# First attention head group of a float32 decoder layer: context blocks first, K and V of a block in turn, first Q from unsplit float32 operands

## The reference, cut to what matters

```
q = layernorm(x) @ wq          # 128 x 4096: 32 query heads of 128, in 8 groups of 4
k = ctx @ wk ; v = ctx @ wv    # 2048 x 1024: one K head and one V head per group
q, k = rope(q), rope(k)        # ctx enters without a norm
scores = q @ k.T + mask ; probs = softmax(scores) ; x = x + (probs @ v) @ wo
```

## Time and profile before

| what | us |
|---|---|
| median of 3 executions (706.46 to 709.02) | 707.11 |
| the profiled execution, its own time | 707.14 |
| its span, first to last instruction | 705.4 |
| TensorE busy in that span | 694.2 (98%) |

### The profile page before, as it was taken

How to read it: one execution, slowest core, us unless ns; L and a number is a source line. 1 busy time by engine, 2 the same in 40 slices (tenths; PEclk the granted TensorE clock), 3 DMA queues, 4 the chain that set the end, 5 groups by cost and what they waited for, 6 DMA issues and landing times. The chain is left out here.

```text
span 705.4 us, 12247 instructions
## 1 busy us (share of the span) xinstructions
PE 694.2 (98%) x4088; PEld 592.4 (84%) x4088; DVE 547.5 (78%) x1180; ACT 391.9 (56%) x601; POOL 299.6 (42%) x151
## 2 busy tenths in 40 slices
PE   8999999999999999999999999999999999999997
PEld 7888888888888888888888888799989898999976
DVE  5988578658748857775874884867999999999984
ACT  4563454536546456454553654553867676767752
POOL 3353223404503513240450440300288887888762
PEclk9999999999999999999999999999999999999999
DMA  9602022021001202202101100781678888788710
GB/s 319 269 28 76 1 74 74 0 74 59 15 15 59 74 0 74 74 0 74 59 15 39 73 22 0 274 355 64 239 270 301 323 306 334 295 334 304 280 52 16
DMA packets 20293, 93.77 MB, mean 133 GB/s; under 512 B 2608, under 2 KB 3760, under 8 KB 11440
## 3 DMA queue, kind: packets, MB, share of 16 engines
q1 hardware_dynamic: 20272, 93.50, 36.0%
HBM read 93.17 MB, written 0.33 MB: 133 GB/s over the span
## 5 line engine op out<-in xcount | busy, mean ns | idle before, releaser
L1562 POOL TENSOR_TENSOR wqo_lo<-wqo_raw,wqo_hi 128x2048 fp32r<-128x2048 f32 x14 | 65.0, 4641 | 163.8 <-ACT wqo_hi L797 163.8
L1230 DVE TENSOR_TENSOR pt_lo<-bank,pt_hi 128x512 fp32r<-128x512 f32 x128 | 87.8, 690 | 48.5 <-ACT pt_hi L875 47.7
L875 ACT ACTIVATE pt_hi<-bank 128x512 fp32r<-128x512 f32 x128 | 75.8, 599 | 54.5 <-PE bank L521 48.9
L1549 POOL TENSOR_TENSOR k_lo<-rope_a,k_hi 128x512 fp32r<-128x512 f32 x32 | 42.7, 1336 | 103.9 <-ACT k_hi L815 103.9
L1595 POOL TENSOR_TENSOR w_out_lo<-w_out_sb,w_out_hi 128x2048 fp32r<-128x2048 f32 x16 | 73.4, 4588 | 21.6 <-ACT w_out_hi L986 21.6
L1138 DVE CUSTOM_DVE_ANT_0 probs<-bank,mask_sb 128x512 f32<-128x512 f32 x128 | 82.0, 685 | 0.1
L1600 POOL TENSOR_TENSOR w_gate_lo<-w_gate_sb,w_gate_hi 128x2048 fp32r<-128x2048 f32 x14 | 64.7, 4623 | 16.7 <-ACT w_gate_hi L978 16.7
L858 ACT ACTIVATE probs<-probs,neg_max 128x2048 f32<-128x2048 f32 x31 | 61.9, 2002 | 3.1 <-DVE neg_max L1128 3.1
L521 PEld LDWEIGHTS bank<-ident_r,probs_r 128*128 128x128 f32 x448 | 48.6, 139 | 15.7 <-DVE pt_lo L1230 3.3
L395 PE MATMUL bank<-pt_hi,v_hi 128*128 128x512 f32 (+1 forms) x144 | 61.0, 424 | 0.0
L655 PE MATMUL bank<-xnT,w_hs_sb 128*128 128x128 f32 x512 | 60.6, 277 | 0.0
(11 more groups left out here) (210 smaller groups left out, 1746.6 us busy)
## 6 DMA issues: line engine op xcount, KB each, us to landing
w_hs_sb<-in_w_hs SPq DMA_DIRECT2D x16, 1024.0 KB, 4.9
w_out_sb<-in_w_out SPq DMA_DIRECT2D x16, 1024.0 KB, 6.3
w_gate_sb<-in_w_gate SPq DMA_DIRECT2D x16, 1024.0 KB, 4.8
wqo_raw<-in_wq SPq DMA_DIRECT2D x8, 1024.0 KB, 4.8
wqo_raw<-in_wo SPq DMA_DIRECT2D x8, 1024.0 KB, 4.8
decay<-decay_rows SPq DMA_DIRECT2D x16, 512.0 KB, 6.8
ctx_raw<-in_ctx_t SPq DMA_DIRECT2D x3, 1024.0 KB, 11.2
wk_raw<-in_wk SPq DMA_DIRECT2D x8, 256.0 KB, 2.5
```

The source lines that it names most:

```text
L875: act.activation(pt_hi[t % 3], ring_b[(t + 1) % 2][:, :], ACT.Copy).then_inc(s["pt_hi_ready"], 1)
L1230: dve.tensor_tensor(pt_lo[t % 3], ring_b[(t + 1) % 2][:, :], pt_hi[t % 3].bitcast(F32), ALU.subtract)\
L1562: pool.tensor_tensor(wqo_lo[:, :, :], wqo_raw[:, :, :], wqo_hi[:, :, :].bitcast(F32), ALU.subtract)\
```

## The change

- **Transfers.** x moves from first place to behind the context's block 1 and the K rope tables 0. wq moves from third place to behind block 3. Block 0 comes in 4 pieces, blocks 1 to 3 in 2 pieces each, wv right after block 0.
- **Weights of group 0.** `wk` and `wv` are split by ACT (`hi`) and DVE (`lo`) in place of POOL. `wq` isn't split at all: Q of group 0 is 4 full float32 matmuls of `xnT` by `wqo_raw`, into another bank.
- **Norm.** Its statistics, scale and transposes move behind K2; the second run of 14 fillers goes, and the first shrinks from 32 to 20.
- **Order on TensorE.** K0 V0 K1 V1 K2, transposes of the norm, V2, a wait for `qx_lo` (the split norm that later groups use), V transposes 0, Q, K3, Q transposes, V transposes 1, V3, V transposes 2. The bank into which the norm is transposed is the one that V transposes 0 write, hence the wait.
- **Order on VectorE and ScalarE** follows this.

The diff's core (renamed semaphores and declarations left out):

```diff
@@ sync
-            sp.dma_start(xres[:, :], x).then_inc(s["x_in"], 16)
             sp.dma_start(wk_raw[:, :, :], wk[0]).then_inc(s["wk_in"], 16)
...
-            for i, two in enumerate(PAIRS):
-                sp.dma_start(ctx_raw[:, 0, two, :], ctx_t[:, two, 0:512]).then_inc(first_ctx_in[i], 16)
-            sp.dma_start(wqo_raw[:, :, :], wq[0]).then_inc(s["wq_in"], 16)
+            for c in range(KC):
+                sp.dma_start(ctx_raw[:, 0, c, :], ctx_t[:, c, 0:512]).then_inc(first_ctx_in[c], 16)
+            sp.dma_start(wv_raw[:, :, :], wv[0]).then_inc(s["wv_in"], 16)
             load_context(1)
-            sp.dma_start(cos_q[:, :], rope_q_cos).then_inc(s["tables_in"], 16)
-            sp.dma_start(sin_q[:, :], rope_q_sin).then_inc(s["tables_in"], 16)
             load_rope_k(0)
-            sp.dma_start(wv_raw[:, :, :], wv[0]).then_inc(s["wv_in"], 16)
+            sp.dma_start(xres[:, :], x).then_inc(s["x_in"], 16)
             load_context(2)
             load_rope_k(1)
             load_context(3)
+            sp.dma_start(wqo_raw[:, :, :], wq[0]).then_inc(s["wq_in"], 16)
@@ tensor
                 if first_head(g):
-                    pe.wait_ge(s["qx_lo_ready"], 1)
...
+                    pe.wait_ge(s["wq_in"], 16)
+                    pe.wait_ge(s["first_xnT_ready"], 1)
+                    for c in range(KC):
+                        last = pe.matmul(first_q_bank[:, :], xnT[:, c, :], wqo_raw[:, c, :], start=c == 0,
+                                         stop=c == KC - 1)
...
+            turn_identity(20, bank[4])
+
+            project_k_block(0, 0)
+            project_v_block(0, 0)
+            project_k_block(0, 1)
+            project_v_block(0, 1)
+            project_k_block(0, 2)
             transpose_norm(1)
-            turn_identity(14, bank[4])
-
-            project_k_block(0, 0)
+            project_v_block(0, 2)
+            pe.wait_ge(s["qx_lo_ready"], 1)
+            transpose_v_block(0, 0)
             project_q(0)
-            project_k_block(0, 1)
-            project_v_block(0, 0)
+            project_k_block(0, 3)
             transpose_q(0)
-            project_k_block(0, 2)
-            project_v_block(0, 1)
-            project_v_block(0, 2)
-            transpose_v_block(0, 0)
-            project_k_block(0, 3)
             transpose_v_block(0, 1)
             project_v_block(0, 3)
             transpose_v_block(0, 2)
@@ scalar
+            act.wait_ge(s["wk_in"], 16)
+            act.activation(wk_hi[:, :, :], wk_raw[:, :, :], ACT.Copy).then_inc(s["wk_hi_ready"], 1)
+            for c in range(KC):
+                act.wait_ge(first_ctx_in[c], 16)
+                ctx_high(0, slice(c, c + 1))
+            act.wait_ge(s["wv_in"], 16)
+            act.activation(wv_hi[:, :, :], wv_raw[:, :, :], ACT.Copy).then_inc(s["wv_hi_ready"], 1)
+            ctx_high_halves(1)
             first_v_copy(0)
-            q_high(0)
-            act.wait_ge(ctx_in[3], 16)
-            ctx_high(3)
+            ctx_high_halves(2)
+            ctx_high_halves(3)
             k_high(0, 0)
...
@@ vector
-                if b == 1:
+                if b == (3 if isinstance(g, int) and g == 0 else 1):
                     dve.wait_ge(s["qT_mm"], g + 1)
...
+                if isinstance(g, int) and g == 0:
+                    src = first_q_bank
+                    dve.wait_ge(s["k_lo_ready"], 2)
@@ gpsimd
             norm_scale(1)
-            split_wk(0)
-            split_wv(0)
             k_low(0)
```

More of the change, by code:

```diff
@@ L271, in build @@
         s = {n: whole.enter_context(nc.semaphore(n)) for n in names}
-        first_ctx_in = [whole.enter_context(nc.semaphore(f"first_ctx_in{i}")) for i in range(2)]
-        ctx_in = [whole.enter_context(nc.semaphore(f"ctx_in{b}")) for b in range(KB)]
+        first_ctx_in = [whole.enter_context(nc.semaphore(f"first_ctx_in{i}")) for i in range(KC)]
+        second_ctx_in = [whole.enter_context(nc.semaphore(f"second_ctx_in{i}")) for i in range(2)]
+        third_ctx_in = [whole.enter_context(nc.semaphore(f"third_ctx_in{i}")) for i in range(2)]
+        fourth_ctx_in = [whole.enter_context(nc.semaphore(f"fourth_ctx_in{i}")) for i in range(2)]
+        half_ctx_in = [None, second_ctx_in, third_ctx_in, fourth_ctx_in]
         rope_k_in = [whole.enter_context(nc.semaphore(f"rope_k_in{b}")) for b in range(KB)]
@@ L433, in project_q @@
                 if first_head(g):
-                    pe.wait_ge(s["qx_lo_ready"], 1)
[L435 to L441, removed]
+                    pe.wait_ge(s["wq_in"], 16)
[3 more added lines that the diff above has]
+                                         stop=c == KC - 1)
+                else:
+                    pe.wait_ge(s["wq_lo_ready"], g)
+                    for c in range(KC):
+                        last = pairs(oq_bank[:, :], qx_hi[:, c, :], qx_lo[:, c, :], wqo_hi[:, c, :], wqo_lo[:, c, :],
+                                     c == 0, c == KC - 1)
                 last.then_inc(s["qproj_ready"], 1)
@@ L445, in transpose_q @@
                 pe.wait_ge(s["qrope_add"], g + 1)
[L446 to L447 removed]
+                pe.wait_ge(s["v_lo_ready"], 1 if first_head(g) else KB * g - 1)
                 for h in range(HG):
@@ L887, in ctx_high @@
                     .then_inc(s["ctx_hi_ready"], 1)
[L889 to L898, removed]
@@ L1274, in first_k_rotate, with first_weight_low @@
                 k_rotate(0, b)
-            ctx_low(0, 1, PAIRS[0])
+            def first_weight_low(raw, hi, lo, hi_done, lo_done):
+                dve.wait_ge(hi_done, 1)
+                dve.tensor_tensor(lo[:, :, :], raw[:, :, :], hi[:, :, :].bitcast(F32), ALU.subtract).then_inc(lo_done, 1)
+            first_weight_low(wk_raw, wk_hi, wk_lo, s["wk_hi_ready"], s["wk_lo_ready"])
+            for c in range(KC):
+                ctx_low(0, c + 1, slice(c, c + 1))
+            first_weight_low(wv_raw, wv_hi, wv_lo, s["wv_hi_ready"], s["wv_lo_ready"])
@@ new lines, in _ @@
+            ctx_low(1, 5, PAIRS[0])
+            ctx_low(1, 6, PAIRS[1])
+            dve.wait_ge(s["x_in"], 16)
+            half_stats(1, 0)
+            half_stats(1, 1)
+            dve.wait_ge(s["norm_stats"], 2)
+            dve.bn_aggr(mean_var[:, :], stats[:, :, :].rearrange("p a b -> p (a b)")).then_inc(s["norm_agg"], 1)
+            first_k_rotate(0)
+            ctx_low(2, 7, PAIRS[0])
+            ctx_low(2, 8, PAIRS[1])
+            dve.wait_ge(s["norm_rstd"], 1)
+            dve.tensor_scalar(xn[:, :], xres[:, :], mean_var[:, 0:1], rstd[:, 0:1], ALU.subtract, ALU.mult)\
+                .then_inc(s["xn_ready"], 1)
@@ L1283, in _ @@
[L1283 to L1288, removed]
+            first_k_rotate(2)
+            v_low(0, 0)
             dve.wait_ge(s["tables_in"], 32)
             q_rotate(0)
-            ctx_low(2, 5, PAIRS[0])
@@ L1543, in split_weight, with k_low @@
                     .then_inc(lo_done, 1)
-            def k_low(g):
-                for b in range(KB):
+            def k_low(g, blocks=range(KB)):
+                for b in blocks:
                     blk = slice(b * 512, (b + 1) * 512)
```

69 lines of the change are left out of this document (36 added, 33 removed).

## The result

The changed kernel takes 708.99 us (median of 20 executions, 707.82 to 710.19) where the kernel before took 708.11 beside it (20 executions, 706.33 to 709.02): a ratio of 1.0021, 95% interval 1.0013 to 1.0029. By that interval the change costs 0.9 to 2.1 us; the two medians alone are 0.9 apart (1.0012), the two means 1.1. The prediction said no change, 707.2. The median lies in its range (705.0 to 709.2) but outside the sum's own (706.1 to 708.2), and a loss was not forecast. Of the 1.8 us between forecast and median, 1.0 lies in the starting value: 707.11 was the median of three executions, and twenty have 708.11. The profiled execution took 709.69 us with a span of 708.0, 2.6 more than before.

The account below looks back on a forecast made before the run. Bounds: TensorE's order, behind it VectorE in the start. +3.6 earlier start, -0.64 Q, -0.36 norm transposes, +0.3 small waits, -2.0 `qx_lo`, -0.95 `k_lo` left nothing; by the mark 707.14 + 0.1, so 707.2 us, range 705.0 to 709.2.

Parts of the forecast that it names:

- the sum's own: Range of the summed time alone, 706.1 to 708.2 us, from GpSimd's meeting with VectorE and uncertain landings and starts.
- head 1: Start of head 1 of the scores on TensorE: predicted at 40.65 us, 40.55 before.
- Earlier start: First K block on TensorE: starts at 6.8 us, ends at 10.0 instead of 13.63, so 3.6 us won.
- VectorE's list: VectorE's work from 13.0 us to `qx_lo`: 12.6 us together, 26.15 with GpSimd's delay, so TensorE waits 2.0.
- GpSimd against VectorE: GpSimd's `k_lo` of block 0 delays VectorE's add of K rotation 1: 0.5 us taken, between 0 and 0.85.
- Q in full float32: Group 0's Q on TensorE: eight records 0.43 us apart, 3.43 against 2.79 split, costing 0.64.
- The last K block: Block 3 of head 0 waits 0.95 us for `k_lo`, ready near 39.5 us.
- From head 1 on: Rest of the program after 40.55 us: the start's difference carried one for one to the end, 707.14 + 0.1.
- the mark: The start of head 1 of the scores in the kernel before, 40.55 us, whose shift was carried to 707.14.
- Rival B: TensorE stays slow longer at the start, through V0: 5.0 us more, 3.0 left, 710.2 us; chance 0.07.
- Rivals A and C: A: VectorE keeps up, 704.2 or half, 705.7, chance 0.22. C: VectorE's chain longer, 708.2 to 710.2, chance 0.09.

Follow-up runs that it names:

- e5_changed_again: The changed kernel run again with no edit, beside the kernel before: 708.41 us (12 executions), ratio 1.0028.

## Why the prediction was wrong

The step that failed is the sentence "A wait of 1.61 us elsewhere did not slow the matmuls after it, so I add nothing for pace." I had read the 0.36 us behind that wait and stopped. The clock falls later than that, in the kernel before as in the changed one. What the runs showed in its place: in the changed kernel's profile Q behind the wait takes 4.73 us where 3.45 were summed, and 3.03 where no fall comes.

| step | predicted | profiled execution above | one without the fall (e5_changed_again) |
|---|---|---|---|
| V2 ends | 24.15 | 24.57 | 24.92 |
| wait for `qx_lo` | 2.00 | 2.07 | 2.08 |
| V transposes 0 | 0.35 | 0.49 | 0.49 |
| Q, to K3's start | 3.45 | 4.73 | 3.03 |
| K3's start to head 1 | 10.70 | 10.90 | 10.89 |
| head 1 | 40.65 | 42.76 | 41.41 |

(V2's end is the start of the V transposes less the wait.)

- *Earlier start.* Right. K0 starts at 6.56 (6.8 predicted) and V0 at 9.57 (10.0). What I left out is a wait at K2: TensorE comes there 0.4 us early and the first half of `ctx_lo` 0.4 late (18.3, not 17.9), so K2 starts 0.52 us behind the pace of V1, 0.36 of it a wait in the trace. By this V2 ends late and not early; of its 0.42, 0.16 is only that the table takes the end of its last record and the sum its pace. In the execution without the fall V2 ends 0.35 later still; K0 waited 0.72 us there for two pieces of `ctx_lo`.
- *VectorE's list.* Right in its order and nearly in its length: statistics start at 13.46 (13.0), `qx_lo` is ready at 26.59 (26.15). The 13.13 us between are the sum's 12.6 and 0.5, but by luck: GpSimd cost 0.6 more, and the rest took 0.6 less, half of it `xn` (0.45 from start to start where I had 0.75). The wait came out right by luck as well: TensorE's list was late by as much.
- *GpSimd against VectorE.* The mechanism was right, the size wrong: I took 0.5, between 0 and 0.85; it was 1.1. I let `k_lo` meet only the add and not the context split behind it, which reads both operands from SBUF as well. My lower end was "if `k_lo` starts 0.4 later, VectorE goes first and loses nothing": VectorE's add went first by 0.02 us and kept its 0.69, and the split behind it lost 1.1. In the changed kernel once more `k_lo` went first by 0.04 us, and the add lost 1.1. The page of the Trainium skill "SBUF — State Buffer", "Who interferes with whom", says that the order of issue decides who blocks. The two traces agree.
- *Q in full float32.* At clock 1.00 the records are 0.43 apart, as summed. By starts Q is shorter (3.03) and K3 longer: its first record is 0.79 long and its second starts 0.64 later, where in the scores it is 0.31, so 0.33 of Q lies in K3's stretch. With the fall it costs 1.70 more.
- *The last K block.* The wait at block 3 is 0.45 where I had 0.95, since head 0 starts later against K3: 7.04 us behind its start, not 6.55, of which 0.33 is the piece of Q. The two nearly cancel.
- *From head 1 on.* I moved the mark and nothing else. The profiled execution loses 0.41 more up to the last head (459.70 against 457.08), of which 0.34 is one weight load of head 1 that waits for VectorE's mask.
- *Rival B* had the right mechanism, TensorE at the lower pace, in the wrong place: I looked for it at the start, where the pace rose as forecast, and not behind the wait that I had just put into the sum. Rivals A and C didn't come.

So of the 2.11 us that head 1 is later than predicted in the profiled execution, 1.28 are Q, 0.42 V2's end, and 0.41 the small terms. Without a fall in Q it is 0.76 later: 0.77 at V2's end and 0.41 in the small terms, less 0.42 at Q.

Over executions the fall in Q comes in about half (6 of 12 where it is the only one), which makes 0.7 to 0.9 us on average. Without it head 1 starts 0.15 us later than before (40.70, wait filled) to 0.86 (41.41, the changed kernel once more). These two add up to 0.9 to 1.8 us, where 0.9 to 2.1 were measured. But the sum isn't closed: counted by the mean clock, the change brings 0.87 falls more per execution, 1.5 us at 1.70 each, and with the later start that is 1.6 to 2.3, while the means of its two sets of executions are 1.1 and 2.1 us above those of the kernel before. What ties the loss to the falls is the run with the wait filled: `qx_lo` still holds TensorE up, the falls are no more frequent than before (4 of 11 executions), and its ratio to the kernel before is 0.9999.

Open is what decides whether the fall comes. All 32 executions of the changed kernel had at least one, and two waits whose falls came by chance, each in half of the executions and on its own, would have left about a quarter without. So the two falls are tied to each other, or the last head's comes more often than before: if Q's comes in half, the 46 falls of the 32 executions leave some 30 for the last head, where the kernel before has 36 in 63. The wait there is as long in both (1.62 and 1.61 us). No run here shows why. Whether the executions with one fall had it in Q or at the last head is seen in one profile only (at the last head).

## What to carry to other kernels

Read a stretch of several microseconds behind a wait of the engine that bounds the kernel, with the granted clock in fine stretches, before calling the wait harmless: it can cost its own length and nearly as much again afterwards (2.07 and 1.70 us here). Where such a loss comes in some executions only, count it over many of them; one profile, or a median of three, can show either case. Ask of each new wait what it is for: this one was for a bank and not for an operand, and another bank took it away. Where a wait must stay, work of no use in it can keep the pace, and a price of one instruction against another on a shared port must be followed to the instructions queued behind.

## What the runs showed of the hardware

- Behind waits of 1.6 and 2.1 us the granted clock fell to 0.50 (1.2 GHz). In the seven falls of the profiles it fell 0.4 to 1.7 us after the engine had resumed, and came back while the engine was busy, 3.9 to 5.1 us after it had resumed. It doesn't come every time: where only the wait ahead of Q was left, 6 of 12 executions had it, and behind the 1.6 us at the last head two profiles show none (no wait, half filling). Behind waits of 0.90 and 0.99, one profile each, there was no fall.
- With 18 or 9 identity transposes in the wait Q kept clock 1.00 in the profile, and with 13 in the wait of the last head all 11 executions of the kernel before had a mean clock of 1.000.
- Beside GpSimd's subtraction VectorE lost 1.1 us whichever of the two came first: on the add when it came second (1.80), on the context split behind the add when the add came first (3.46 in place of 2.35). Beside the rotation products, with one operand in PSUM, neither lost anything (0.69 and 1.30).
- The kernel before has a spread of its own, at a mean clock of 1.000: 705.39 to 707.26 on the second chip. In the profiled execution of the run that filled its last head the first context halves took 7.5 us to land, against 5.3 in the trace of before, and head 1 started at 42.50 instead of 40.55 with the same code in the start.
